# Two-layer adaLN network: gates fixed on columns, row spreading per element, and the seam into attention rearranged

## The chip, the cores and the metric

The kernel runs on one core of one Trainium2 chip. The metric is the device time of one execution in microseconds (us), as the median of several runs. The engines are TensorE (PE; its weight loads are shown as PEld), VectorE (DVE), ScalarE (ACT), GpSimd (POOL) and SyncE (SP, which here only issues transfers). Each runs its own list of instructions in order, and they wait for one another through semaphores.

## What is computed

Eight batch elements of 512 tokens with 128 channels pass two blocks. All numbers are float32.

```
mod = (silu(c) @ wmod).reshape(8, 6, 1, 128)          # for each layer: sa, ca, ga, sb, cb, gb
ga  = (2*(ga >= 0) - 1) * maximum(abs(ga), 0.25)      # the same for gb: "fixing" a gate
# layer 0
h = layernorm(x)*(1 + ca) + sa;  x = x + ga * rwkv(h)              # time mixing, WKV scan over 512 tokens
h = layernorm(x)*(1 + cb) + sb;  x = x + gb * (quant(h) @ quant(W).T + bias)   # 6-bit blocks of 32
# layer 1
h = layernorm(x)*(1 + ca) + sa;  x = x + ga * attention(h)
h = layernorm(x)*(1 + cb) + sb;  x = x + gb * tanh(x_t @ wo.T + c_final @ uo.T + bo)
```

The attention has 16 heads in four groups of four. Each query sees three sets of keys: latent keys (causal), 32 tokens selected by the highest score of `h @ w_imp`, and "window" keys (causal). Three gates per element, a softmax over the mean of `h @ w_gate`, weight the three. Part of each query and key is rotated (rope).

## The kernel before

**Setup.** SyncE loads the weights. TensorE forms `mod` with channels on partitions (`modc`, 12 rows of 8 elements). Layer 0 also needs gates and shifts as rows, the same on all partitions. For that TensorE multiplies, for each of the eight elements, silu(c) repeated over 128 columns with the modulation weights (L1612 to L1618); ScalarE copies 4x128 columns to `modrow` (`row_read`, L814) and VectorE copies layer 1's output gate to `garow1` (`row_reads`, L1159). VectorE then fixes the gates in their row form by `row_gates` (L1166): four passes over 8x128 columns each for `modrow[:, :, 0]`, `modrow[:, :, 3]` and `garow1`; `ffn_rows` (L1171) adds one and forms the bias row `brow` for all elements.

**Layer 0.** A loop written out over b = -2 to 9 on each engine holds element b+1 in its mixing part, b in its WKV part, b-1 in its FFN and b-2 in its passage to attention. VectorE's order in a step is: `wkv(b)` (starts with the scan at L1212, ends with the product at L1232), `quantised_ffn(b-1)` (ends with the codes at L1089), `maxima(b+1)`, `norm_ffn(b)`, `keep_moments(b-2)`, moments of `norm_mix(b+2)`, `norm_attention(b-1)` (L1247). ScalarE: `normed_mix(b+1)` (L820), `mix_input(b+1)` (L836), `normed_attention` and `attention_input(b-2)`, `receptance(b+1)` (L842), `ffn_input(b-1)`, `exponentials(b+1)` (L848 to L854), `normed_ffn(b)`. GpSimd: `gate_wo(b)` (L638), `decode(b-1)` (L651), deviations (L625 to L632), `modulate_ffn(b)`, `gate_ffn(b)`. TensorE: transposes (L1623), projections (L1639, L1640), `project_out` (L1648), `ffn` (L1661, L1666), one score row (L1679).

Into this loop a table `SLOTS` (L107) places the projections of attention's first group, which all pass one shared PSUM bank: each `fill` on TensorE waits for the `read` of the one before. The top-32 choice of elements 0 to 3 is made in step 6; reading the rank, normalising the tokens (`tokens`, L1293) and picking (L1298) follow in step 7, `ks`, the projection of selected keys and its rotation (L1318 to L1327), in step 8. GpSimd rotates the first group's keys (`rope(start, "k", 0)`, L663 to L676) in step 7, ahead of step 8's `decode(7)`. Steps 8 and 9 end element 7: its FFN, normalisation, passage, score, the three gate products (`gate_logits`, L1855) and `vs`.

**Transfers.** SyncE moves rotated and other parts to the group buffers in an order written out by hand: queries' rotated halves, unrotated queries, rotated window keys, unrotated window keys, latent keys (`lay_group`, 28 transfers, 32 with the shared key), then `lay_selected` (12). Both queries' and keys' rotated parts count on one semaphore, `s_lx`.

**Attention.** A unit is one head and one or two tiles of queries against one key set; 24 units make a group: 12 on latent and selected keys, 12 on window keys. `Turn(FIRST)` is group 0 of element 0, then a hardware loop runs seven full turns of four groups and a last one of three. In a unit TensorE makes scores (L1822), VectorE masks and finds the maximum (L1425), ScalarE exponentiates (L980), TensorE transposes (L1849), VectorE or ScalarE moves the result, TensorE multiplies with the values (L1783). In the first turn TensorE waits at unit 0 for all transfers of the group; VectorE waits before it for all GpSimd steps of layer 0 (L1550). `FIRST` also holds the top-32 choice of elements 4 to 7 (from unit 2 on) and the softmax of the gates.

## Time and profile before

| | |
|---|---|
| median of 3 runs | 2014.3 us (2013.28 to 2017.04) |
| profiled execution: time, span | 2014.44 us, 2012.6 us |
| TensorE busy | 1822.4 us (91%) |
| VectorE busy | 1287.3 us (64%) |
| ScalarE busy | 1173.0 us (58%) |
| GpSimd busy | 677.5 us (34%) |
| mean granted clock of TensorE | 0.947 |

Rows of a time line give the start in us from the span's start, the duration in us of the merged instructions, the engine, the line of the kernel, the operation, output and input names and sizes, the count, and in brackets the idle time before and what ended it. Names such as `arena` cover many buffers; the line tells which. Rows of the table by stage give the stretch, its length, then the busy us (and instructions) of PE, PEld, DVE, ACT and POOL, the granted clock of TensorE as a share of 2.4 GHz, the share of the DMA engines and GB/s. The profile has one execution only, on the one core.

### The profile page before, as it was taken

The page shows a single profiled execution, that of the slowest core. Times are in us where ns is not written, and L with a number is a line of the kernel's source. Part 1 is how long each engine was busy: PE and PEld are TensorE (multiplying, and loading weights), DVE is VectorE, ACT ScalarE, POOL GpSimd, SP SyncE. Part 2 cuts the span into 40 slices and gives each one's busy share as a digit, 9 for nine tenths or more (in the row PEclk, how much of TensorE's full clock was granted, in tenths as well). Part 3 has the DMA queues.
Part 4 walks back from the last instruction along what each step waited for, and adds up shares of the span by engine and source line. Part 5 has one row for each costly group of instructions (what it writes and reads, how often), then busy time and mean ns, then how long its engine had stood idle before and what let it go on. Part 6 is the DMA issues. An engine that isn't in the chain of part 4 may idle for free.

```text
span 2012.6 us, 38380 instructions
## 1 busy us (share of the span) xinstructions
PE 1822.4 (91%) x10672; PEld 1076.1 (53%) x10672; DVE 1287.3 (64%) x3817; ACT 1173.0 (58%) x3572; POOL 677.5 (34%) x698
## 2 busy tenths in 40 slices
PE   5575789999999999999999999999999999999996
PEld 3332445555555555655555555555655556555552
DVE  6999666656566666666666656665666666666672
ACT  3464356656565656666565656665666566666651
POOL 1456433343233323333343333332333234333300
PEclk8778589999999999999999999999999999999998
DMA  4001021111011111121112111120111111211101
GB/s 157 1 0 27 15 58 38 38 43 52 24 40 39 47 35 38 42 48 48 39 38 52 48 26 47 35 54 20 44 43 38 49 38 38 52 48 38 37 1 42
DMA packets 71346, 81.42 MB, mean 40 GB/s; under 512 B 29521, under 2 KB 37842, under 8 KB 70994
## 3 DMA queue, kind: packets, MB, share of 16 engines
q1 hardware_dynamic: 71122, 78.74, 15.4%
q8 instruction: 103, 1.69, 0.4%
q14 instruction: 121, 0.99, 0.2%
HBM read 7.90 MB, written 2.10 MB: 5 GB/s over the span
## 4 chain that ended last, share of the span: by engine, by line
issue 49%; PE 21%; POOL 19%; DVE 8%; ACT 2%; POOLq 1%; DMA 0%; DVEq 0%; SPq 0%; ACTq 0%
PE bank L1822 6%; PE bank L1849 3%; POOL arena L674 3%; PE bank L1783 3%; POOL arena L676 3%; POOL arena L663 2%; POOL arena L673 2%; POOL arena L664 2%; PE bank L1688 2%; POOL arena L672 1%; POOL arena L712 1%; DVE arena L1225 1%; PE bank L1683 1%; PE bank L1746 1%; PE bank L1729 1%
## 5 line engine op out<-in xcount | busy, mean ns | idle before, releaser
L1425 DVE CUSTOM_DVE_ANT_0 arena<-bank,W 128x512 f32<-128x512 f32 (+3 forms) x1024 | 480.6, 488 | 523.0 <-PE bank L1822 363.9
L980 ACT ACTIVATE arena<-arena 128x512 f32<-128x512 f32 (+3 forms) x1024 | 570.4, 560 | 369.5 <-DVE arena L1425 366.6
L1822 PE MATMUL bank<-arena 96*128 96x512 f32 (+6 forms) x2048 | 716.5, 452 | 15.9 <-issue 14.5
L1822 PEld LDWEIGHTS bank<-arena 96*128 96x128 f32 x2048 | 350.2, 192 | 190.5 <-issue 154.5
L1849 PE MATMUL bank<-W,arena 128*128 128x128 f32 x2560 | 430.0, 282 | 0.1
L1849 PEld LDWEIGHTS bank<-W,arena 128*128 128x128 f32 x2560 | 301.4, 144 | 222.1 <-issue 183.3
L1436 DVE COPY arena<-bank 128x512 f32<-128x512 f32 (+1 forms) x512 | 318.5, 622 | 78.6 <-PE bank L1849 75.8
L712 POOL TENSOR_TENSOR arena<-arena,one 128x512 f32<-128x512 f32 x64 | 66.8, 1044 | 812.2 <-DVE arena L1393 806.2
L1783 PE MATMUL bank<-arena 128*32 128x256 f32 (+1 forms) x3072 | 223.2, 363 | 1.9 <-DVE arena L1436 1.8
L980 ACT ACTIVATION_READ_ACCUMULATOR arena<-arena 128x1 f32 x1024 | 197.3, 193 | 0.0
L959 ACT ACTIVATE arena<-bank 128x384 f32<-128x384 f32 x256 | 124.6, 487 | 94.4 <-PE bank L1849 92.6
L1783 PEld LDWEIGHTS bank<-arena 128*32 128x32 f32 x3072 | 61.0, 108 | 184.8 <-issue 158.9
L663 POOL TENSOR_TENSOR arena<-arena,W 128x512 f32<-128x512 f32 x64 | 69.9, 1092 | 205.4 <-ACT arena L898 205.4
L974 ACT ACTIVATE arena<-bank 128x32 f32<-128x32 f32 (+1 forms) x384 | 65.2, 205 | 105.0 <-DVE arena L1425 103.8
L1688 PE MATMUL bank<-arena,W 128*128 128x512 f32 x192 | 103.1, 619 | 21.9 <-ACT arena L898 21.8
L1687 PE MATMUL bank<-arena,LW 96*128 96x512 f32 x192 | 103.3, 620 | 2.8 <-ACT arena L898 2.7
L672 POOL TENSOR_TENSOR arena<-arena 128x512 f32<-128x512 f32 x64 | 81.4, 1272 | 56.1 <-DMA arena<-arena 50.0
L1623 PE MATMUL bank<-W,arena 128*128 128x128 f32 x160 | 34.0, 351 | 71.6 <-ACT arena L820 45.3
L898 ACT ACTIVATE arena<-bank 128x512 f32<-128x512 f32 x128 | 76.2, 595 | 33.4 <-PE bank L1687 19.4
L1425 DVE DVE_READ_ACCUMULATOR2_ANT arena<- 128x1 f32 x1024 | 84.8, 83 | 0.0
L676 POOL TENSOR_TENSOR arena<-arena 128x512 f32<-128x512 f32 x64 | 81.3, 1270 | 5.0
L674 POOL TENSOR_TENSOR arena<-arena,W 128x512 f32<-128x512 f32 x64 | 78.0, 1220 | 0.0
(265 smaller groups left out, 2221.0 us busy)
## 6 DMA issues: line engine op xcount, KB each, us to landing
arena<-arena SPq DMA_DIRECT2D x896, 64.0 KB, 2.0
arena<-arena SPq DMA_DIRECT2D x64, 128.0 KB, 2.6
W<-wide SPq DMA_DIRECT2D x1, 3730.0 KB, 13.4
X<-x SPq DMA_DIRECT2D x8, 256.0 KB, 5.5
out<-arena SPq DMA_DIRECT2D x8, 256.0 KB, 2.3
arena<-arena SPq DMA_DIRECT2D x96, 16.0 KB, 1.9
LW<-lat SPq DMA_DIRECT2D x1, 768.5 KB, 14.3
arena<-mods SPq DMA_DIRECT2D x1, 768.0 KB, 4.5
```

Of the source, the lines that this page charges most:

```text
L663: step(pool.tensor_tensor(rt[:, 2], rt[:, 0], w("cos"), ALU.mult))
L674: step(pool.tensor_tensor(rt[:, 1], rt[:, 1], w("cos"), ALU.mult))
L676: pool.tensor_tensor(stX2, rt[:, 0], rt[:, 1], ALU.add).then_inc(s_rope, 1)
L959: A(turned(turn, k), turned_bank(turn, k), ACT.Copy).then_inc(s_pa, 1)
L980: done = A(here, here, ACT.Exp, bias=nmax[:, c:c + 1], scale=-1.0, accum_out=lsum[:, c:c + 1])
L1425: last = v.tensor_tensor_reduce(Pb[:, s % 4, at_p:at_p + n], bank[turn.score_bank(s)][:, at + lo:at + lo + n], w("mask", T - n), -1.0, 3e3 ...
L1436: CP(turned(turn, k), turned_bank(turn, k)).then_inc(s_pd, 1)
L1687: return MM(dst[:], LW[0:QL, col:col + P], latT[0:QL], start=True, stop=True)
L1688: return MM(dst[:], w("wink", col, P), hTc, start=True, stop=True)
L1783: last = MM(bank[5][rows, low * 2 * P:low * 2 * P + n], V[a][turn.g(q) % 2][:, c, rows], PT[low][:, h, c * 2 * P:c * 2 * P + n], start=(c ...
L1822: last = MM(B_[:, at:at + lo + n], query(t), Kb[a][g % 2][0:QD, h, skip:skip + lo + n], start=True, stop=True)
L1849: last = pe.transpose(bank[3 + k % 2][:, n * P:(n + 1) * P], Pb[:, k % 4, c * P:(c + 1) * P], ident)
```

## The change

Three groups of edits.

1. Gates. VectorE fixes the gates in `modc` (columns 2, 5, 8 and 11 at once, 4x8 columns) and forms `brow` there with channels on partitions; the bias weight is a new column of the packed weights, so its own transfer goes. The eight row products of the setup, `row_reads`, `row_gates` and `ffn_rows` go. `rows(b)` on TensorE now spreads one element's four columns through products with the identity (eight passes of 128 columns), for element 0 before the loop and for b+1 at the end of step b; `modrow` has two places in place of eight. ScalarE's `row_read(b)` follows `mix_input(b+1)`. `garow1` is spread in two halves in steps -1 and 0 (`output_gates`), read by ScalarE. The FFN's bias comes from `brow` times the identity.
2. Seam. The loop ends at b = 8. Element 7's last normalisation, its transposes (`z3T`), the scores of elements 4 to 7 (`score`), the gate products (`gates`) and `vs` become tasks of the first attention turn, at units 2, 4, 7 and 12; the top-32 choice there starts at unit 6 in place of 2, and the rank moves from 14 to 17. The slots of steps 6 to 8 change: rank at the end of 6, selected tokens and keys at the top of 7, `x2k`, `nk3`, `nk1`, `vl` after them.
3. Rotation. `rope(start, "k", 0)` moves behind `decode(7)` in step 8. SyncE lays the first group's selected keys, latent keys and then rotated keys; `s_lx` is split in two, and TensorE waits for the window keys only at a group's unit 12.

```diff
-        extra = [(14, "rank")] if first else [(12, "z4T"), (14, "gf"), (15, "gi"), (19, "gc")]
+        extra = [(2, "z3T"), (4, "score"), (7, "gates"), (12, "vs"), (17, "rank")] if first else [(12, "z4T"), (14, "gf"), (15, "gi"), (19, "gc")]
...
-         (6, "mid"): "vw", (6, "out"): "x1k", (6, "end"): "x2k",
-         (7, "mid"): "rank", (7, "out"): "nk3", (7, "end"): "sel",
-         (8, "top"): "ks", (8, "out"): "nk1", (8, "end"): "vl", (9, "out"): "vs"}
+         (6, "mid"): "vw", (6, "out"): "x1k", (6, "end"): "rank",
+         (7, "top"): "sel", (7, "next"): "ks", (7, "out"): "x2k", (7, "end"): "nk3",
+         (8, "top"): "nk1", (8, "mid"): "vl"}
...
@@ SyncE
-            lay_group(Turn(START), 0)
+            lay_queries(start, 0)
+            lay_latent_queries(start, 0)
             sp.wait_ge(s_ksd, 1)
             lay_selected()
+            lay_latent_keys(start, 0)
+            lay_keys(start, 0)
...
@@ GpSimd
                 if 0 <= b < B:
-                    if b == 0:
-                        pool.wait_ge(s_rowg, 1)
+                    pool.wait_ge(s_rowsa, b + 1)
                     gate_wo(b)
                 if 0 <= b - 1 < B:
                     decode(b - 1)
+                if b == B:
+                    rope(start, "k", 0)
...
-                if b == 7:
-                    rope(start, "k", 0)
...
@@ ScalarE
             def row_read(b):
                 act.wait_ge(s_rows, b + 1)
-                A(modrow[:, b].rearrange("p a c -> p (a c)"), bank[4 + b % 2][:], ACT.Copy).then_inc(s_rowsa, 1)
+                if b > 1:
+                    act.wait_ge(s_wdg, b - 1)
+                A(modrow[:, b % 2].rearrange("p a c -> p (a c)"), bank[4][:], ACT.Copy).then_inc(s_rowsa, 1)
...
+                    if turn.first and s == 1:
+                        normed_attention(B - 1)
...
-            for b in range(5):
-                row_read(b)
             act.wait_ge(s_setup, 1)
-            normed_mix(0)
-            for b in range(5, B):
-                row_read(b)
-            for b in range(-2, B + 2):
+            row_read(0)
+            for b in range(-2, B + 1):
                 if 0 <= b + 1 < B:
-                    if b + 1 > 0:
-                        normed_mix(b + 1)
+                    normed_mix(b + 1)
                     mix_input(b + 1)
+                if 0 < b < B:
+                    row_read(b)
+                if 0 <= b < 2:
+                    output_gates(b)
...
@@ VectorE
-            gate_fix(modc[:, 11], gmx, gsm)
             step.settle()
-            TS(gsm, gmx, 1.0, None, ALU.mult).then_inc(s_setup, 1)
+            gate_fix(modc[:, 2:12:3], ta, tb)
+            step.settle()
+            step(TS(brow, modc[:, 5], vec("b0"), None, ALU.mult))
+            step.settle()
+            CP(cells[:, 1:2], cells[:, 0:1]).then_inc(s_setup, 1)
...
-            for b in range(-2, B + 2):
-                if b == -1:
-                    row_gates(modrow[:, :, 0])
+            for b in range(-2, B + 1):
+                if b == 7:
+                    read(start, "rank", 0)
+                    for j in range(NT):
+                        last = pick(0, j)
+                    last.then_inc(s_zc, 1)
                 if 0 <= b < B:
                     wkv(b)
+                if b == 7:
+                    read(start, "ks", 0)
...
@@ TensorE
-            for b in range(B):
-                if b >= 2:
-                    pe.wait_ge(s_rowsa, b - 1)
-                    pe.wait_ge(s_rowsd, b - 1)
-                MM(bank[4 + b % 2][:], silu[:, b:b + 1].to_broadcast([P, P]), wmod[:, 0, 2 * P:6 * P], start=True, stop=True)
...
+            def spread_rows(dst, columns):
+                for n, column in enumerate(columns):
+                    last = MM(dst[:, n * P:(n + 1) * P], column.to_broadcast([P, P]), ident, start=True, stop=True)
+                return last
+
+            def rows(b):
+                if b > 0:
+                    pe.wait_ge(s_var2, b)
+                spread_rows(bank[4], [modc[:, n, b:b + 1] for n in range(2, 6)]).then_inc(s_rows, 1)
...
-                            pe.wait_ge(s_lx, (p0 + q) * (16 * 4 * HG) + 16 * 4 * HG)
+                            pe.wait_ge(s_lq, (p0 + q) * (16 * 2 * HG) + 16 * 2 * HG)
...
+                        if s % GU == RU:
+
+                            pe.wait_ge(s_lx, (p0 + q) * (16 * 2 * HG) + 16 * 2 * HG)
+                            pe.wait_ge(s_lk, (p0 + q) * (16 * HG) + 16 * HG)
...
-                if 0 <= b - 2 < B:
-                    score(b - 2)
+                if 0 <= b - 2 < HALF_B:
+                    score(bank[5], b - 2).then_inc(s_sc, 1)
+                if 0 <= b < B - 1:
+                    rows(b + 1)
+                if -1 <= b < 1:
+                    output_gates(b + 1)
                 slot(b, "end")
-            gate_logits()
```

## Rows read from the trace of the kernel before

**Rows 1.** busy time by stage (columns: see time and profile)
```profile
64.00:208.00 144.00, 96.53 (x290) 48.23 (x290) 135.12 (x287) 73.76 (x154) 78.45 (x108) 0.75 0.04 10
...
263.66:312.28 48.62, 45.68 (x254) 27.27 (x255) 38.06 (x111) 29.77 (x94) 15.36 (x13) 0.96 0.19 50
```

**Rows 2.** time line of TensorE, unit 24 (start, us, engine, line, out<-in, count)
```profile
312.28 1.02 PE L1822 MATMUL bank<-arena 96*128 96x512 f32 x2
```

**Rows 3.** time line of the setup, GpSimd, ScalarE, VectorE
```profile
16.07 0.20 POOL L632 TENSOR_TENSOR small<-small 128x4 f32<-128x4 f32 x1
...
23.21 1.63 ACT L820 ACTIVATE arena<-X,small 128x128 f32<-128x128 f32 x4
...
37.57 1.04 ACT L854 ACTIVATE arena<-arena 128x1024 f32<-128x1024 f32 x1
...
40.06 1.19 DVE L1212 TENSOR_TENSOR_SCAN arena<-arena 128x512 f32<-128x512 f32 x1
```

**Rows 4.** time line from element 0's WKV scan to element 1's
```profile
43.59 1.65 ACT L820 ACTIVATE arena<-X,small 128x128 f32<-128x128 f32 x4 [4.98 <-POOL small L632]
...
56.16 0.69 DVE L1237 TENSOR_TENSOR arena<-X,bank 128x512 f32<-128x512 f32 x1 [0.72 <-PE bank L1648]
...
59.25 0.66 DVE L1124 TENSOR_SCALAR arena<-garow 128x1024 f32<-128x1024 f32 x1
...
59.30 1.04 ACT L854 ACTIVATE arena<-arena 128x1024 f32<-128x1024 f32 x1
...
63.17 1.22 DVE L1212 TENSOR_TENSOR_SCAN arena<-arena 128x512 f32<-128x512 f32 x1
```

**Rows 5.** time line of element 2's step
```profile
87.68 1.11 PE L1623 MATMUL bank<-W,arena 128*128 128x128 f32 x4 [4.54 <-ACT arena L820]
...
88.84 0.78 ACT L836 ACTIVATE arena<-bank,modc 128x512 f32<-128x512 f32 x1 [1.21 <-PE bank L1623]
...
92.83 0.41 POOL L638 TENSOR_TENSOR arena<-W,arena 128x128 f32<-128x128 f32 x1
...
96.43 0.69 DVE L1232 SCALAR_TENSOR_TENSOR arena<-arena 128x512 f32<-128x512 f32 x1
```

**Rows 6.** time line of VectorE, element 7's step
```profile
208.31 1.19 DVE L1212 TENSOR_TENSOR_SCAN arena<-arena 128x512 f32<-128x512 f32 x1
...
222.44 0.18 DVE L1309 COPY rankT<-bank 128x32 f32<-128x32 f32 x1
...
222.66 1.84 DVE L1293 TENSOR_SCALAR arena<-X,stat 128x128 f32<-128x128 f32 x4
...
224.42 0.67 DVE L1298 TENSOR_SCALAR arena<-W,rankT 128x32 f32<-128x32 f32 x4
```

**Rows 7.** time line from element 7's codes to unit 0 of attention
```profile
234.72 0.69 DVE L1089 TENSOR_TENSOR arena<-arena,small 128x512 fp8e4<-128x512 f32 x1
...
235.95 1.09 POOL L663 TENSOR_TENSOR arena<-arena,W 128x512 f32<-128x512 f32 x1
...
243.01 1.05 POOL L651 TENSOR_TENSOR arena<-arena,small 128x512 f32<-128x512 fp8e4 x1
...
249.27 0.69 DVE L1247 TENSOR_TENSOR X<-arena,bank 128x512 f32<-128x512 f32 x1 [6.31 <-PE bank L1666]
...
251.79 1.02 POOL L630 TENSOR_TENSOR small<-small,cst 128x4 f32<-128x4 f32 x1
...
253.71 8.11 SPq L569 DMA_DIRECT2D arena<-arena  x12
...
263.66 2.05 PE L1822 MATMUL bank<-arena 96*128 96x512 f32 x2 [1.39 <-ACT arena L943]
...
266.04 0.69 DVE L1425 CUSTOM_DVE_ANT_0 arena<-bank,W 128x512 f32<-128x512 f32 x1 [10.99 <-PE bank L1822]
```

**Rows 8.** time line of TensorE, gate products and four transposes of attention
```profile
258.70 3.58 PE L1859 MATMUL bank<-W,hsum 128*128 128x3 f32 x16
...
270.08 0.60 PE L1849 MATMUL bank<-W,arena 128*128 128x128 f32 x4
```

More of the change, by code:

```diff
@@ L665, in rope @@
                 step.settle()
-                use = (turn.p0 + k) * 2 + (0 if kind == "q" else 1)
-                if not (isinstance(use, int) and use == 0):
-                    pool.wait_ge(s_lx, use * (16 * 2 * HG))
+                p = turn.p0 + k
+                use = p * 2 + (0 if kind == "q" else 1)
+                if kind == "k":
+                    pool.wait_ge(s_lq, p * (16 * 2 * HG) + 16 * 2 * HG)
+                elif turn.tasks is not START:
+                    pool.wait_ge(s_lx, p * (16 * 2 * HG))
                 if turn.g(k) == 0 and kind == "q":
@@ L922, in read @@
                     last = A(latT, G[:], ACT.Copy)
+                elif name == "z3T":
+                    last = A(HT[:, (B - 1) * T:], G[:], ACT.Identity, bias=modc[:, 6, B - 1:B],
+                             scale=modc[:, 7, B - 1:B], accum_out=hsum[:, B - 1:B])
+                    last.then_inc(s_ga, 1)
+                    act.wait_ge(s_ga, turn.read("z3T"))
+                    act.sem_inc(s_h3, 1)
+                    return
                 elif name == "vs":
@@ L1306, in read @@
                     v.wait_ge(s_gd, turn.read("o2", k))
+                elif name == "score":
+                    step(CP(top, G[0:B]))
+                    CP(marked, G[0:B]).then_inc(s_gd, 1)
+                    v.wait_ge(s_gd, turn.read("score"))
+                elif name == "gates":
+                    CP(gates[:].rearrange("p b n -> p (b n)"), G[:, 0:3 * B]).then_inc(s_gd, 1)
+                    v.wait_ge(s_gd, turn.read("gates"))
+                    gates_shifted()
                 elif name == "rank":
@@ L1514, in _ @@
                     top_ranked()
+                    for j in range(NT):
+                        tokens(0, j)
                 if 0 <= b - 1 < B:
                     quantised_ffn(b - 1)
-                if b == 7:
-                    read(start, "rank", 0)
-                    for j in range(NT):
-                        tokens(0, j)
-                    for j in range(NT):
-                        last = pick(0, j)
-                    last.then_inc(s_zc, 1)
-                if b == 8:
-                    read(start, "ks", 0)
                 if 0 <= b + 1 < B:
                     maxima(b + 1)
-                if b == -1:
-                    row_gates(modrow[:, :, 3])
-                    ffn_rows()
                 if b == 0:
@@ L1707, in fill @@
                         last = pe.transpose(G[:, j * B:(j + 1) * B], top[:, j * P:(j + 1) * P], ident[0:B, 0:B])
+                elif name == "z3T":
+                    pe.wait_ge(s_z3, B)
+                    last = turn4(G, z3)
+                elif name == "score":
+                    for b in range(HALF_B, B):
+                        last = score(G, b)
+                elif name == "gates":
+                    pe.wait_ge(s_h3, B)
+                    for b in range(B):
+                        last = MM(G[:, 3 * b:3 * b + 3], hsum[:, b:b + 1].to_broadcast([P, P]), w("gate"), start=True, stop=True)
                 elif name == "sel":
@@ L1853, in attend @@
                         fill(turn, *task)
-            def gate_logits():
-                pe.wait_ge(s_h3, B)
-                pe.wait_ge(s_var3, B)
-                for b in range(B):
-                    last = MM(bank[6][:, 3 * b:3 * b + 3], hsum[:, b:b + 1].to_broadcast([P, P]), w("gate"), start=True, stop=True)
-                last.then_inc(s_gl, 1)
             start = Turn(START)
@@ L1867, in slot @@
                     fill(start, name, 0)
-            for b in range(-2, B + 2):
+            rows(0)
+            for b in range(-2, B + 1):
                 if b == 3:
```

179 lines of the change are left out of this document (80 added, 99 removed).

## Prediction

> **What bounds the kernel now.** I read the table by stage first, then the time lines of single engines where it pointed. In layer 0 (64 to 208 us) VectorE is busy 135.1 of 144 us and TensorE 96.5, at a granted clock of 0.75; in the first turn of attention (263.66 to 312.28) TensorE is busy 45.7 of 48.6 us at 0.96 and bounds, with VectorE at 38.1 [rows 1]. Between them lies a stretch in which a chain of single steps runs: VectorE ends its last moments at 251.3 and has nothing of weight until 266.04 [rows 7]. The whole change lies before unit 24 of attention, which starts at 312.28 [rows 2]; the 1700 us behind it have the same work in the same order, so I carry whatever is won at unit 24 to the end. The profiled execution took 2014.44 with a span of 2012.6; the median of the runs shown is 2014.3, so a saving is taken off either alike.
>
> Let element b be one of the eight batch elements, and "W(b)" the start of its WKV scan on VectorE (L1212). Four points carry the sum: W(0) 40.06 [rows 3], W(1) 63.17 [rows 4], W(7) 208.31 [rows 6], unit 24.
>
> **Setup, W(0).** Before, TensorE spreads eight elements' gates one after another, and ScalarE normalises element 0 only after five row copies, at 23.21, though its deviation was ready at 16.27 [rows 3]. After it, one element is spread (four columns in two passes of 128 each, about 2 us: an estimate from twice the 1.11 of four transposes of 128 columns in one pass each, cold [rows 5]; it begins at 13.3 and is done before the normalisation) and one copy of 0.6 follows. VectorE's four fixing steps now cover 4x8 columns in place of 8, and one small product and a copy replace the last step: +0.3. So the normalisation starts at 16.6 and ends at 18.3. From there to the last exponential I take element 1's chain, in which TensorE was at 0.5: its normalisation started at 43.59 and took 1.65, its last exponential ended at 60.34, 15.1 later [rows 4]. W(0) is then at 33.4: 6.7 won. Element 0's own chain in the old kernel, mostly at the upper clock, took 13.8 from 24.84 to 38.61, 1.6 of which was waiting behind row products: 12.2, W(0) at 30.5, 9.6 won. I take the cold value, since TensorE will have stood for some 3 us before the transposes, and after 4.5 us of standing the transposes at 87.68 took 1.11, where four of them in attention take 0.60 [rows 5, 8].
>
> The Trainium skill (TensorE: Matmul & The Clock Gate, section HAM oscillation) says that a stream of matmuls which pauses between bursts falls back to the lower clock. By that rule 33.4 is right and the spread products are no lasting warm-up; without it W(0) would be 30.5. The trace agrees in kind: the granted clock is 0.75 over layer 0 [rows 1].
>
> **Gates of the rows, W(1).** The fixing of the output gates (four passes over 1024 columns and a marker, 59.25 to 63.17) goes: 3.9 [rows 4]. The two fixings of modrow and the bias product fall into the stretch already counted, up to W(0). The 0.72 for which VectorE waited before 56.16 for element 0's projection goes too [rows 4], since TensorE is done sooner. Is something else late then? W(1) on VectorE would be 33.4 + (59.25 - 40.06 - 0.72) = 51.9; element 1's exponentials end 16.75 after its normalisation begins [rows 4], which ScalarE can start at 33.4: 50.2. VectorE stays last by 1.7. W(1) moves by 6.7 + 3.9 + 0.7 = 11.3.
>
> **Elements 1 to 6.** Each step gains on TensorE eight passes (2.1 cold), behind the projection and FFN of the element, waiting for the FFN moments; on ScalarE a copy of 0.6; VectorE has nothing new. Behind the waiting TensorE stand only the next element's transposes, whose input comes over 4 us later from GpSimd and ScalarE (normalisation of element 2 after VectorE's moments: 1.25 + POOL + 1.65). On ScalarE the copy stands behind mix_input and before receptance, which waits for r, three projections of 512 columns later. On GpSimd gate_wo now waits at the head of a step for that copy, with decode behind it: in element 2's step mix_input ended at 89.6, so the copy at 90.2; gate_wo ran at 92.83 [rows 5]. Cost nothing, with 2.6 us of cover, and more for decode, whose codes come after rwkv; if the cover is gone it costs what the copy is late. No row shows the pair, so I bound it at -0.5 to +0.5 per step, six steps: -3 to +3. I take 0, VectorE being 94% busy.
>
> **Element 6's step, W(7).** The tokens (1.84) move from element 7's step to this one; reading the rank (0.18) and the picks (0.67) move ahead of W(7) [rows 6]. TensorE reaches the rank transposes only after the FFN, the spread of element 7 (2) and ScalarE's read of a key projection; VectorE in the meantime has the residual addition and moments, 2.0 by the piece from 249.27 to the deviation whose third step is at 251.79 [rows 7]: a wait of 0.8, estimated from 2 + 0.6 + 0.2 - 2.0. Together 3.5 later. W(7) is 208.31 - 11.3 + 3.5 = 200.5.
>
> **End of layer 0.** In times of the old trace from W(7) on: rank, tokens and picks (222.44 to 225.0, [rows 6]) go, the selected keys' rotation comes in their place (seven operations of 128 columns; by the 0.2 to 0.67 of the picks and of such a row 2 to 3, taken as the same 2.6); its 24 products now run under the WKV scan. So element 7's codes end at 235.41 as before. Decode then no longer queues behind the key rotation (from 235.95): it starts at 235.9 in place of 243.01 [rows 7]. From decode's start to the last residual addition took 6.26 (249.27); but TensorE must first do nk1, the last-but-one transposes and vl, each cold: walking these, I get 245.8 and not 242.2. The moments are then at 247.8. GpSimd meanwhile rotates the keys (7.0, to 243.9; more if VectorE is in its way) and makes the deviation, whose last counted step ended 1.53 after the moments (at 252.81). VectorE still waits for all GpSimd steps before attention: it starts unit 0 at 249.4 in place of 266.04. The old start hung on SyncE: the transfers that needed the rotated keys came first, then from 253.71 the 12 of the selected keys, on whose copy unit 0 waited [rows 7]. After: the selected keys are ready at about 223 (rank's 222.44, less some 2 of the quantisation ahead of it, plus 2.6), their 12 issues (8.1) end at 231, the latent keys follow nk1's read at 236.7 and have landed by 241.5. The rotated keys' 12 transfers (0.67 each) follow rotation from 243.9 to 252; unit 12 needs them some 25 us after unit 0. So TensorE starts unit 0 at 245.8, right behind the last FFN, in place of 263.66, and stands two to three units ahead of VectorE.
>
> **First attention turn.** It takes over z3T, four scores, the gate products and vs. At the upper clock: score pairs like unit 24's pair of 512 columns, 1.02 each, 3.9 with overlap [rows 2]; 16 gate products at half of the cold 3.6; z3T and vs at most like four transposes, 0.60, and half of it [rows 8]: together 6.5. TensorE stood 2.9 us in this turn [rows 1], so little hides; the least is 6.5 - 2.9 = 3.6, the most (all at 1.2 GHz) 13. On ScalarE a normalisation of 1.65 stands before the exponentials of unit 1: +1. Ranking moves four units later, with one unit and not two before the rank transposes. The old turn lasted 48.6 from TensorE's start and 46.2 from VectorE's. From 245.8: 245.8 + 48.6 + 6.5 = 300.9; from 249.4: 249.4 + 46.2 + 6.5 + 1 = 303.1. I take 302. Unit 24 comes 10.3 before 312.28 on the old clock, on top of the 7.8 by which W(7) moves.
>
> **Sum.** 11.3 - 3.5 + 10.3 = 18.1 won. Span 1994.5; time 2014.3 - 18.1 = 1996.2.
>
> **Rivals.** (1) The moved work costs double in the first turn: it waits for element 7's chain, VectorE (38.1 of 48.6 us busy there [rows 1]) and the late rank, or runs at the lower clock. 7 us less: 2003. For it: little slack of either engine; against: a granted clock of 0.96 over this turn. (2) All short ends: setup warm (2.9), TensorE's clock up at the end of layer 0 so that the last addition is at 242.2 (3.6), waits of the turn filled (2.9): 9.4 more, 1987. (3) The change doesn't do what it says at the start of attention: VectorE's wait for all GpSimd steps, or a transfer, holds unit 0 so that half of the 17 us stays: 2004.5. (4) Slower: the row copy in front of gate_wo and decode. If the copy ends later than rwkv (96.43 + 0.69 in element 2's step) TensorE's projection waits, and each us is paid in seven steps. Copy end to rwkv is 6.9 us; gate_wo takes 0.4 of it. From 6.5 + 18.1/7 = 9.1 us of delay per step the kernel is slower than before; with 10.5 us (a copy stuck behind the exponentials) it is 7 x 4.0 - 18.1 = 9.9 slower, 2024. Against: ScalarE is in order and has nothing long between mix_input and the copy.
>
> **How the numbers follow.** Forecast (1991 to 2000) 0.55; (1) 0.17; (2) 0.13; (3) 0.09; (4) 0.03; a rest of 0.03 for no net change. The range is 1987 to 2005: it takes in (1) to (3) and the bounds of the spread. Some 0.2% (4 us) is what a measurement of this kernel can tell from no change. Faster 0.93, within 0.04, slower 0.03.
>
> **What would show it.** W(0) at 33 (30.5 if warm), W(1) at 52, W(7) at 200, VectorE's unit 0 at 249.4 - 7.8 = 241.6, unit 24 at 294; periods between W(1) and W(6) unchanged within 0.5; no wait of TensorE for GpSimd's L638 in steps 1 to 7; SyncE's selected-key transfers ahead of the rotated keys. I am wrong if the first turn lasts over 60 us, if the step periods grow, or if the groups after unit 24 change.

## The result, and the profile after

The changed kernel takes 2029.07 us (2025.57 to 2031.45, five runs) against 2014.3 of the kernel before (2010.06 to 2020.21, five runs): the ratio is 1.0068, 95% interval 1.0045 to 1.0091. It is slower; I had forecast 1996.2. The profiled execution took 2025.57 with a span of 2023.5, 10.9 more than before. Three executions among the later runs took far longer (8660 us in e1, 5094 in e11, 2328 of the kernel before beside e9 to e12) and are in no ratio.

The seam came out nearly as forecast. The time lines of VectorE and TensorE after, at the starts of the WKV scans of elements 0, 1 and 7, unit 0 on either engine, and unit 24:

```profile
33.18 1.23 DVE L1227 TENSOR_TENSOR_SCAN arena<-arena 128x512 f32<-128x512 f32 x1 [5.40 <-ACT arena L877]
51.42 1.19 DVE L1227 TENSOR_TENSOR_SCAN arena<-arena 128x512 f32<-128x512 f32 x1
...
199.71 1.22 DVE L1227 TENSOR_TENSOR_SCAN arena<-arena 128x512 f32<-128x512 f32 x1
...
234.96 1.54 PE L1846 MATMUL bank<-arena 96*128 96x512 f32 x2
...
239.09 0.69 DVE L1447 CUSTOM_DVE_ANT_0 arena<-bank,W 128x512 f32<-128x512 f32 x1 [1.88 <-issue]
...
295.85 1.02 PE L1846 MATMUL bank<-arena 96*128 96x512 f32 x2
```

The same points of the kernel before are 40.06 [rows 3], 63.17 [rows 4], 208.31 [rows 6], 263.66 and 266.04 [rows 7] and 312.28 [rows 2]. Unit 24 comes 16.4 us sooner. Then the gain is lost and more. This is the table by stage, one row for each full turn of attention, counted from VectorE's first instruction in it (columns: stretch, length, busy us of PE, PEld, DVE, ACT and POOL, granted clock, DMA share, GB/s), of before:

```profile
313.29:528.43 215.14, 205.30 (x1281) 122.61 (x1280) 132.75 (x414) 133.32 (x421) 72.89 (x68) 0.99 0.17 42
528.43:743.48 215.05, 205.51 (x1276) 122.98 (x1272) 132.64 (x413) 133.20 (x421) 72.89 (x68) 0.98 0.17 42
...
sum 1699.31, PE 1606.27 PEld 957.07 DVE 1038.36 ACT 1030.22 POOL 546.77; mean PE 200.78 PEld 119.63 DVE 129.79 ACT 128.78 POOL 68.35
```

and of after:

```profile
296.85:511.68 214.83, 203.59 (x1274) 121.76 (x1274) 133.70 (x415) 133.20 (x422) 79.12 (x68) 0.99 0.17 42
511.68:729.96 218.28, 207.36 (x1273) 123.64 (x1273) 133.75 (x413) 133.32 (x421) 79.12 (x68) 0.98 0.17 41
...
1387.46:1607.56 220.10, 208.06 (x1273) 123.65 (x1272) 133.86 (x413) 133.20 (x421) 79.14 (x68) 0.97 0.17 41
...
sum 1726.65, PE 1619.18 PEld 961.73 DVE 1047.84 ACT 1030.24 POOL 593.38; mean PE 202.40 PEld 120.22 DVE 130.98 ACT 128.78 POOL 74.17
```

From the start of the first full turn on, the same work takes 27.3 us more (1726.65 against 1699.31). Two things stand in these rows. GpSimd is busy 79.1 us a turn in place of 72.9, with as many instructions (68). And the first full turn is as quick as before, every later one 3.2 to 5.2 us longer, which points at the loop's jump back (this holds for one of the two causes only: in e7 below the first full turn is long too). For 12.9 of the 27.3 us TensorE is busy with the same matmuls, so it ran at the lower clock more often; for 14.4 it stands.

### The profile page after: what moved, and what is told of

The parts are those of the page before. It is cut to its first block, busy times and chain, and to the rows that moved or that the text cites. A ratio compares the mean times of both kernels' runs of the same rounds, so it can differ in the third digit from the quotient of the medians.

```text
span 2023.5 us, 38502 instructions
## 1 busy us (share of the span) xinstructions
PE 1825.5 (90%) x10720; PEld 1083.9 (54%) x10720; DVE 1280.0 (63%) x3786; ACT 1173.5 (58%) x3574; POOL 724.3 (36%) x698
## 4 chain that ended last, share of the span: by engine, by line
issue 47%; PE 20%; POOL 19%; DVE 1%; ACT 1%; POOLq 1%; DVEq 0%; ACTq 0%
PE bank L1846 6%; PE bank L1873 3%; POOL arena L693 3%; POOL arena L692 3%; POOL arena L680 3%; PE bank L1806 3%; POOL arena L695 2%; POOL arena L679 2%; PE bank L1701 2%; POOL arena L731 1%; POOL arena L691 1%; PE bank L1696 1%; PE bank L1769 1%; PE bank L1752 1%; POOL arena L717 1%
## 5 line engine op out<-in xcount | busy, mean ns | idle before, releaser
L1846 PE MATMUL bank<-arena 96*128 96x512 f32 (+6 forms) x2048 | 721.2, 454 | 14.5 <-issue 14.5
L1846 PEld LDWEIGHTS bank<-arena 96*128 96x128 f32 x2048 | 353.1, 193 | 190.7 <-issue 154.6
L1806 PE MATMUL bank<-arena 128*32 128x256 f32 (+1 forms) x3072 | 227.4, 364 | 2.7 <-issue 1.4
L1806 PEld LDWEIGHTS bank<-arena 128*32 128x32 f32 x3072 | 62.2, 109 | 188.8 <-issue 164.0
L679 POOL TENSOR_TENSOR arena<-arena,W 128x512 f32<-128x512 f32 x64 | 81.6, 1276 | 191.6 <-ACT arena L921 191.6
L921 ACT ACTIVATE arena<-bank 128x512 f32<-128x512 f32 x128 | 76.2, 595 | 44.9 <-PE bank L1700 29.8
L691 POOL TENSOR_TENSOR arena<-arena 128x512 f32<-128x512 f32 x64 | 81.4, 1272 | 48.1 <-DMA arena<-arena 42.8
L693 POOL TENSOR_TENSOR arena<-arena,W 128x512 f32<-128x512 f32 x64 | 89.1, 1392 | 0.0
## 6 DMA issues: line engine op xcount, KB each, us to landing
W<-wide SPq DMA_DIRECT2D x1, 3730.0 KB, 13.4
LW<-lat SPq DMA_DIRECT2D x1, 768.5 KB, 14.3
```

The costliest lines, as they stand in the source:

```text
L679: step(pool.tensor_tensor(rt[:, 2], rt[:, 0], w("cos"), ALU.mult))
L693: step(pool.tensor_tensor(rt[:, 1], rt[:, 1], w("cos"), ALU.mult))
L1806: last = MM(bank[5][rows, low * 2 * P:low * 2 * P + n], V[a][turn.g(q) % 2][:, c, rows], PT[low][:, h, c * 2 * P:c * 2 * P + n], start=(c ...
L1846: last = MM(B_[:, at:at + lo + n], query(t), Kb[a][g % 2][0:QD, h, skip:skip + lo + n], start=True, stop=True)
```

## Two suspects in code that the change never touched

**GpSimd's rotations.** Groups of GpSimd by line from 500 to 1600 us (count | busy us, mean ns | idle before), before:

```profile
L672 POOL TENSOR_TENSOR arena<-arena 128x512 f32<-128x512 f32 x40 | 50.9, 1272 | 34.3 <-DMA arena<-arena 30.2 <-POOL arena L664 4.1
L663 POOL TENSOR_TENSOR arena<-arena,W 128x512 f32<-128x512 f32 x40 | 43.7, 1092 | 127.1 <-ACT arena L898 127.1
```

and after:

```profile
L679 POOL TENSOR_TENSOR arena<-arena,W 128x512 f32<-128x512 f32 x40 | 51.0, 1276 | 121.1 <-ACT arena L921 121.1
L691 POOL TENSOR_TENSOR arena<-arena 128x512 f32<-128x512 f32 x40 | 50.9, 1272 | 32.0 <-DMA arena<-arena 28.6 <-POOL arena L680 3.4
```

Three of the four products of a rotation, which read cosines or sines from the packed weights W, went from 1092 to 1276 ns, and the fourth from 1204 to 1385; the subtraction, which reads two of the rotation's own buffers, stayed at 1272. From the start of the first product to that of the second it is 1050 ns before and 1234 after, so this is more than a way of recording. Nothing in those lines was edited. But the bias became an eleventh column among the vectors of W, and every column behind it, cosines and sines too, moved by 4 bytes. ScalarE's read at L921 fills the rotation's buffers, so it comes after the rotation before it; TensorE waits for that read 20.4 us in this window, in place of 13.5.

VectorE has one operation that slows down as well, a sum of two buffers that reads nothing of W (before, after):

```profile
L1408 DVE TENSOR_TENSOR arena<-arena 128x512 f32<-128x512 f32 x20 | 15.4, 769 | 0.0
L1430 DVE TENSOR_TENSOR arena<-arena 128x512 f32<-128x512 f32 x20 | 21.7, 1083 | 0.0
```

It makes up most of the 9.5 us by which VectorE is busier in the sums above. The half of its instructions that run beside one of GpSimd's products went from 0.84 to 1.35 us. It is hardly what costs the time: in the fastest version of all, e15, it takes 1107 ns. Why it slows down is open.

**TensorE behind the jump.** The time line of TensorE over the start of the second full turn. Before:

```profile
738.53 0.55 PE L1849 MATMUL bank<-W,arena 128*128 128x128 f32 x3
741.27 1.48 PE L1822 MATMUL bank<-arena 96*128 96x512 f32 x2 [2.20 <-issue]
742.69 1.08 PE L1783 MATMUL bank<-arena 128*32 128x256 f32 x8
```

After:

```profile
725.01 0.55 PE L1873 MATMUL bank<-W,arena 128*128 128x128 f32 x3
727.77 2.07 PE L1846 MATMUL bank<-arena 96*128 96x512 f32 x2 [2.22 <-issue]
729.77 0.64 PE L1806 MATMUL bank<-arena 128*32 128x256 f32 x1
730.56 1.08 PE L1806 MATMUL bank<-arena 128*32 128x256 f32 x7 [0.16 <-issue]
```

Each jump back costs a stand (2.2 us here, 2.2 to 2.8 at the six jumps) in which TensorE waits for nothing that the profile shows. Behind it the kernel before runs on; the changed one does three matmul passes and stands once more, though the eight passes of L1806 are issued in one go. The queues of the DMA section that load instructions (packets, MB) say what it is. Before, after:

```profile
q8 instruction: 103, 1.69, 0.4%
```

```profile
q8 instruction: 110, 1.80, 0.4%
```

## Experiments

**e1 to e4: the offset alone.** Unused columns behind the vectors move the rest of W, here for e1 (e2: before with 11, e3: after with 12, e4: before with 12 columns in all):

```diff
-WIDE = [("c", 2 * B), ("vecs", 11), ("ident", P), ("wkT", P), ("wvT", P), ("wrT", P), ("woT", P), ("ffn", P),
+WIDE = [("c", 2 * B), ("vecs", 26), ("ident", P), ("wkT", P), ("wvT", P), ("wrT", P), ("woT", P), ("ffn", P),
...
+    cols += [np.zeros((P, 15), np.float32)]
     cols += [np.eye(P, dtype=np.float32)]
```

> The changed kernel with 15 unused columns behind the eleven vectors of the packed weights W: every later column of W lies 64 bytes further than in the kernel before, and not 4 bytes as in the changed kernel. Theory A (offset of the operands: the one added column moved the cosines and sines by 4 bytes, and GpSimd's products with them went from 1.092 to 1.276 us): the products take 1.09 again, a full turn of attention lasts 215 us in place of 218 to 220, the group sequence is the old one and the 16.4 us won at unit 24 reach the end: 1997 to 2000 us. Rival B (the split waits of TensorE and the new order of SyncE's transfers slow the turns): turns stay at 218 to 220 and the time at 2029. Rival C (other places of the stage buffers or of the code): as B.

> The kernel before with one unused column behind the ten vectors of W, nothing else: the 4 byte shift alone. Theory A: GpSimd's products with cosines and sines take 1.276 in place of 1.092 us, full turns last 218 to 220 in place of 215, and the kernel takes 2036 to 2046 us. Rivals B and C: 2014 us, turns 215.

> The changed kernel with one more unused column: later columns of W are 8 bytes further than before. Open which alignment matters. If GpSimd reads in words of 8 bytes (A8): products 1.09 and 1997 to 2000 us. If operands must share a place within a line of 16 or 64 bytes (A64): products stay at 1.27 and the time at 2029. Rivals B and C: 2029, with 1.09 or 1.27 alike.

> The kernel before with two unused columns: 8 bytes. A8: products 1.09, 2014 us. A64: products 1.27, 2036 to 2046. Rivals B and C: 2014.

| kernel | shift of W | product L663/L679 | full turns 2 to 6 | us | ratio to before |
|---|---|---|---|---|---|
| after | 4 B | 1276 ns | 218.3 to 220.1 | 2029.07 | 1.0068 (1.0045 to 1.0091) |
| e1 after | 64 B | 1093 ns | 217.6 to 219.2 | 2010.01 | 0.9989 (0.9975 to 1.0003) |
| e2 before | 4 B | 1274 ns | 213.7 to 220.3 | 2039.25 | 1.0134 (1.0117 to 1.0151) |
| e3 after | 8 B | 1272 ns | 219.6 to 222.1 | 2032.03 | 1.0089 (1.0064 to 1.0115) |
| e4 before | 8 B | 1272 ns | 218.5 to 220.7 | 2041.31 | 1.0147 (1.0129 to 1.0166) |

The one column makes the kernel before 1.3% slower by itself: theory A is right about its cause, and words of 8 bytes are not the rule. But e1 is not the 1997 to 2000 that I expected. Its products are quick again, its first full turn takes 213.5 us, and the next ones still 217.6 to 219.2. The second stand is there, at 1.0 to 1.4 us behind three of the six jumps and 0.2 to 0.4 behind the other three:

```profile
723.44 0.55 PE L1873 MATMUL bank<-W,arena 128*128 128x128 f32 x3
726.12 1.12 PE L1846 MATMUL bank<-arena 96*128 96x512 f32 x2 [2.13 <-issue]
727.17 0.45 PE L1806 MATMUL bank<-arena 128*32 128x256 f32 x1
728.91 1.08 PE L1806 MATMUL bank<-arena 128*32 128x256 f32 x7 [1.29 <-issue]
```

**e5 to e8: the place of the loop.** Instructions that only raise an unused semaphore, ahead of TensorE's first wait:

```diff
+            for _ in range(20):
+                pe.sem_inc(s_pad, 1)
             pe.wait_ge(s_silu, 1)
```

> The changed kernel with the 64 byte shift of the 64B run, and 20 instructions on TensorE that only raise an unused semaphore, issued while TensorE waits for the first data. The 64B run had GpSimd's products at 1.09 us again, but its full turns behind the first still lasted 217 to 219 us: behind each jump back of the attention loop TensorE stands for 2.1 us, as before, then does three matmul passes, stands again for 1.0 to 1.3 us with no releaser, and runs at the lower clock for up to 11 us. Theory D (code place: TensorE's loop begins 12 instructions ahead of the end of a block of instruction memory, so that a second block must be fetched after the jump; the added instructions before the loop moved it there): 20 more instructions put the loop's start 8 into a block; the second stand goes, full turns last 213.5 to 215 us, 1995 to 1999 us in all. Rival E (the split waits or SyncE's order make the turns longer): as the 64B run, 2010 us.

> The kernel before with 89 such instructions on TensorE ahead of its first wait: its attention loop then begins at the same instruction number as the changed kernel's. Theory D: a second stand of about 1.2 us behind each jump back, turns 217 to 219 from the second on, GpSimd's products at 1.09, 2014 + 6 x 2 to 3 = 2024 to 2034 us. Rival E: 2011 us, turns 215.

> The changed kernel with the 20 instructions on TensorE alone (cosines and sines still 4 bytes off). Theories A and D together: GpSimd's products 1.276, no second stand, 2029 less what the stand cost (12 to 18 us): 2011 to 2017 us. If the two costs don't add, up to 2029.

> The kernel before with 25 such instructions: the loop's start stands at the same place within blocks of 64 instructions as in the changed kernel, and at another within blocks of 128 or 256. A second stand behind the jump (turns 217 to 219): blocks of 64. None (turns 215, 2011 us): blocks of at least 128.

e5 takes 1994.81 us, ratio 0.9937 (0.9917 to 0.9958): the second stand is gone, q8 has 104 packets, and the turns are those of before within 1 us, the sixth is 2.0 shorter (time line of TensorE behind a jump, then the row of the third full turn):

```profile
724.00 1.17 PE L1849 MATMUL bank<-arena 96*128 96x512 f32 x2 [2.36 <-issue]
725.10 1.08 PE L1809 MATMUL bank<-arena 128*32 128x256 f32 x8
```

```profile
726.08:941.07 214.99, 205.65 (x1277) 123.24 (x1274) 132.56 (x413) 133.19 (x421) 72.89 (x68) 0.98 0.17 42
```

e6, the reverse, takes 2031.82, ratio 1.0104 (1.0080 to 1.0128), with 109 packets in q8, six more than before, one for each jump. Not all of it is the loop: the 89 instructions hold TensorE's first matmul until 14.42 us (6.42 before), and the first full turn starts 6.6 later (319.91 against 313.29). From there to the end it takes 1710.4 us against 1699.3: 11.1 for the place of the loop, as in e1 (1711.2). The second stand is seen behind three of the six jumps (0.7 to 1.3 us). e8 took 2013.47 in one run, with 103 packets and turns of 214.9 to 216.8 and no second stand, so the blocks are larger than 64 instructions.

e7 misses the 2011 to 2017: 2018.92, ratio 1.0052 (1.0035 to 1.0070). That is 0.2% better than the changed kernel, with intervals that overlap, where e5 is 0.5% better than e1. The traces, one execution of each version, show the two costs side by side, from the start of the first full turn to the end, for e1 (the loop's place alone) and e7 (the offset alone):

```profile
297.35:2008.50 1711.15, 1613.54 (x9903) 958.24 (x9902) 1038.93 (x3216) 1030.26 (x3245) 547.00 (x509) 0.98 0.16 40
296.69:2015.90 1719.21, 1615.34 (x9903) 966.62 (x9902) 1047.22 (x3216) 1029.30 (x3244) 592.75 (x509) 0.98 0.16 40
```

With neither (e5) it is 1697.8 us, with both (the changed kernel) 1726.6. So the loop's place alone costs 13.4, the offset alone 21.4, and both together 28.9 and not 34.8: the two costs don't add in full. The offset needs no jump: e7's first full turn takes 218.0 us where e5's takes 216.1. At the jump shown above, TensorE came into the changed kernel's loop at the lower clock (L1846 took 2.07 us and not 1.12), so that the second block arrived before it was needed but for 0.16 us; the stand was covered by slowness that was paid for anyway. That is how it goes in general: the fourth pass behind a jump starts 2.5 to 2.9 us after the first at all six jumps of the changed kernel and of e1, and 1.1 to 2.0 us after it in the kernel before, e5 and e7. How much of this is seen as a stand depends on the clock of the three passes.

**The clock behind a stand.** The granted clock behind the jump shown, in windows of 2 us of the kernel before (columns as above):

```profile
741.00:743.00 2.00, 1.73 (x6) 0.50 (x10) 0.00 (x0) 0.00 (x0) 0.00 (x0) 0.72 0.06 16
743.00:745.00 2.00, 2.00 (x12) 1.03 (x5) 1.12 (x4) 0.42 (x1) 0.00 (x0) 0.50 0.01 4
745.00:747.00 2.00, 2.00 (x13) 0.71 (x12) 0.84 (x4) 0.99 (x3) 1.04 (x1) 0.92 0.00 0
```

and the first and last windows of the low stretch in e1:

```profile
727.00:728.00 1.00, 0.63 (x2) 0.14 (x2) 0.00 (x0) 0.00 (x0) 0.00 (x0) 0.70 0.02 8
...
737.00:738.00 1.00, 1.00 (x10) 0.34 (x10) 0.70 (x2) 0.00 (x0) 0.00 (x0) 0.68 0.07 16
```

Before, the clock is at its lower level for 3.4 us (2 x (0.28 + 0.50 + 0.08) = 1.7 us of work at full clock); in e1, with a second stand of 1.3 us, for three times as long, 5.1 us of work. So at this jump the stand came with up to 3.4 us more of lost clock. Other jumps differ: the stretch is 3.4 us at four of the six jumps before and 6.8 at the other two, 6.8 at four jumps of e1 and 10.2 at two, and 3.4 at all six of e5. From the first full turn to the end e1 has TensorE busy 7.2 us longer than e5 and standing 6.2 us longer.

**e9: which offset.** A probe behind the last transfer of the kernel before, with the other engines done, 40 lines of this form with other offsets each:

```diff
+                after_one(TTp(at(2048, 0), at(0, 0), at(1024, 1), ALU.mult))
```

> The kernel before, and behind its last transfer a probe on GpSimd alone, with every other engine done: products of two 128x512 float arrays, each line with one set of offsets of the two inputs and the output, in floats from three bases that stand at the same place of a 64 byte line, 4 times each. Adds some 250 us at the end, which only the probe takes. If the relative place of the inputs decides (R): offset 6 of the second input (the 24 bytes that cosines stood from the staging buffers in the kernel before) takes 1.09 us, 7 and 8 and 0 take 1.27, and (6, 6) takes 1.27 like (0, 0). If the place within a line of one input alone decides (S): the first input's offset or the second's changes it, and (6, 6) is like (0, 6). If neither is seen with the engines idle, it was contention with another engine (C): all lines take the same.

Groups of GpSimd by line; second input at offset 0, 1, 2, 3, 4 and 7 floats (L816 to L823), first input at 1 and 2 (L833, L834), output at 2 (L841), both inputs at 6 (L847):

```profile
L816 POOL TENSOR_TENSOR arena<-arena 128x512 f32<-128x512 f32 x4 | 5.0, 1262 | 0.3
L817 POOL TENSOR_TENSOR arena<-arena 128x512 f32<-128x512 f32 x4 | 4.4, 1091 | 0.3
L818 POOL TENSOR_TENSOR arena<-arena 128x512 f32<-128x512 f32 x4 | 4.4, 1091 | 0.3
L819 POOL TENSOR_TENSOR arena<-arena 128x512 f32<-128x512 f32 x4 | 5.0, 1262 | 0.3
L820 POOL TENSOR_TENSOR arena<-arena 128x512 f32<-128x512 f32 x4 | 5.0, 1260 | 0.3
L823 POOL TENSOR_TENSOR arena<-arena 128x512 f32<-128x512 f32 x4 | 5.0, 1262 | 0.3
L833 POOL TENSOR_TENSOR arena<-arena 128x512 f32<-128x512 f32 x4 | 5.0, 1258 | 0.3
L834 POOL TENSOR_TENSOR arena<-arena 128x512 f32<-128x512 f32 x4 | 4.4, 1092 | 0.3
L841 POOL TENSOR_TENSOR arena<-arena 128x512 f32<-128x512 f32 x4 | 5.0, 1262 | 0.3
L847 POOL TENSOR_TENSOR arena<-arena 128x512 f32<-128x512 f32 x4 | 5.0, 1262 | 0.3
```

R holds. All 40 lines obey one rule: with the second input 1 or 2 floats ahead of the first modulo 4 floats (16 bytes), the product takes 1.09 us; at 0 or 3 it takes 1.26 (from start to start 1.17 and 1.34). The output's place plays no part, and the difference is the same with the other engines idle. In the kernel before the cosines stood 6 floats on (2 modulo 4, quick); the bias column made it 7, one more makes 8, both slow. One or two columns more leave the buffers behind W where they are: in the compiled program of the kernel before W ends 8 bytes short of the next buffer.

**e10, e11, e13: no jump at all.** The attention loop written out seven times, on TensorE (e10), on all engines (e11), and on all engines in the kernel before (e13):

```diff
-            with pe.Fori(0, B - 1) as i:
+            for i in range(B - 1):
```

> The changed kernel with the 64 byte shift and TensorE's attention loop written out seven times, no jump: theory D taken to its end. Each of six jumps cost a stand of 2.1 us and, behind it, 3.4 us at the lower clock (1.7 us of work), in e5 as in the kernel before. If fetching without a jump is hidden and no other engine's own jump takes its place: 1994.8 - 6 x 3.8 = 1972. If the other engines' jumps (VectorE and ScalarE still loop) hold TensorE nearly as long: 1985 to 1995. If straight code of 24000 instructions is fetched too slowly: over 1995, with stands everywhere.

> The same with the attention loop written out on all five engines. Theory D to its end: 1968 to 1974 us, no stand at the turn's boundary. If the fetching of all five engines' code gets in the way of each other or of the transfers: over 1980.

> The kernel before with the attention loop written out on all five engines, as in e11 for the changed one. Theory (the change wins 16 to 19 us ahead of unit 24 and nothing behind it): 1973 + 18 = 1991 us (1988 to 1993), and the difference to e11 at the end is that at unit 24. Rival (the changed kernel's turns are better or worse by themselves too): the difference grows or shrinks from turn to turn.

e10: 1988.3, ratio 0.9881 (0.9852 to 0.9909); TensorE's stands turned into waits for VectorE, which still jumps (waits of VectorE, 500 to 1600 us: total, times, longest):

```profile
DVE gtc L1586 <- issue: 15.9, 6, 2.7
```

e11: 1973.28, ratio 0.9810 (0.9781 to 0.9839), full turns of 209.9 to 213.5 and no stand, as theory D has it. e13: 1982.12, ratio 0.9859 (0.9833 to 0.9884), better than the 1988 to 1993 expected. So the change is worth 0.5% here, by ratios whose intervals just overlap. By the profiled executions the changed kernel is 15.0 us ahead at the start of the first full turn (296.92 against 311.94) and 9.8 at the end (1970.7 against 1980.5): 5 us go on the way. From that start on TensorE does the same 9903 passes in 1594.5 us of busy time against 1590.6: 3.9 of the 5.2 are the lower clock. This pair was to show whether the turns are worth the same in both kernels; the difference shrinks, as the rival said.

**e12 and e16: two terms of the sum.** e5 with the rotation back in front of the decoding, and e5 with TensorE's wait for the rotated and window keys back at a group's first unit:

```diff
-                if b == B:
-                    rope(start, "k", 0)
...
+                if b == 7:
+                    rope(start, "k", 0)
```

```diff
-                        if s % GU == RU:
+                        if s % GU == 0:
```

> The 64 byte, 20 instruction version with one edit undone: GpSimd rotates the first group's keys before the last element's decoding, as in the kernel before. Theory (the decoding is on the path at the end of layer 0, as the prediction has it): decode starts 5 to 7 us later, TensorE's unit 0 and the end move by 4 to 7 us: 1999 to 2002 us. Rival (the first turn waits for the ranks later on and takes it up): 1995 to 1997.

> The 64 byte, 20 instruction version in which TensorE waits for the rotated keys' transfers ahead of a group's first unit, as in the kernel before, and not ahead of its thirteenth. In e5 these transfers were issued until 253.2 and unit 0 began at 232.3. Theory of the prediction (the split lets unit 0 start early): unit 0 at about 255, the end 10 to 20 us later: 2005 to 2015. Rival (the first turn's wait for the ranks and its other work hide it): under 2000. Later groups have their keys long before, so turns stay at 215.

e12: 1997.92, ratio 0.9940 (0.9924 to 0.9956), between my two numbers, and not to be told from e5's 0.9937. In its trace unit 0 is 4.5 us later than in e5 (236.79 against 232.28) and unit 24 6.3 later (299.68 against 293.41), but e5 then spends 3.4 us of work at the lower clock in its first full turn where e12 loses 1.7. The order of rotation and decoding is worth 0 to 3 us at the end, which these runs can't tell from nothing. e16: 2005.4, ratio 0.9977 (0.9960 to 0.9994): the split is worth 0.4%. TensorE stands at unit 0:

```profile
241.44 2.04 PE L1849 MATMUL bank<-arena 96*128 96x512 f32 x2 [8.54 <-DMA arena<-arena]
```

I had expected unit 0 at 255: I read the end of a merged row of 24 transfers, of which the last belong to the next group.

**e14, e15: the rule used.** The second and fourth of the rotation's four buffers 4 bytes further on, so that all six operations are of the quick kind, in e5 (e14) and in e11 (e15):

```diff
-        rt = cv(4, T)
+        rt_a, _, rt_b, _, rt_c, _, rt_d, _ = (cv(n) for n in (T, 1, T, 15, T, 1, T, 15))
+        rt = (rt_a, rt_b, rt_c, rt_d)
```

> The 64 byte, 20 instruction version with the second and the fourth of GpSimd's rotation buffers 4 bytes further on, so that in every operation of a rotation the inputs stand 4 or 8 bytes apart modulo 16. By the probe's rule all six operations take 1.09 us: L692's and L696's subtraction and addition fall from 1.27, a rotation is 0.36 us shorter. If each 0.18 us is worth what the four products' 0.18 were worth (3.3 us a turn for 0.74 us a rotation): up to 1.6 a turn, 1983 us. If a rotation at 7 us is already early enough for TensorE: 1994 to 1995.

> The same buffers in the changed kernel with all loops written out (e11): the fastest version that the runs point to. 1973 less 0 to 12: 1961 to 1973.

```profile
L693 POOL TENSOR_TENSOR arena<-arena 128x512 f32<-128x512 f32 x41 | 44.8, 1092 | 31.3 <-DMA arena<-arena 28.2 <-POOL arena L682 3.1
L697 POOL TENSOR_TENSOR arena<-arena 128x512 f32<-128x512 f32 x41 | 44.7, 1091 | 3.2
```

Subtraction and addition take 1.09 in place of 1.27 (e14). e14: 1988.18, ratio 0.9885 (0.9869 to 0.9902), 0.5% better than e5. e15: 1964.76, ratio 0.9763 (0.9746 to 0.9779), the fastest version, 2.4% below the kernel before. e14 falls between its two expectations (1983, and 1994 to 1995), e15 inside its range.

## Why the prediction was wrong, point by point

- **W(0), W(1).** Forecast 33.4 and 52, measured 33.18 and 51.42. That W(0) fits this well is in part luck: the normalisation starts 0.6 us late (17.22), and from its end to the last exponential it takes 14.3 us, not the 15.1 of a cold chain or the 12.2 of a warm one. Of the six pairs of projection passes the first two are cold (2.08 and 1.82 us), the other four take 1.02.
- **Elements 1 to 6.** Forecast as before within 0.5 a step. W(1) to W(6) took 111.4 us (110.5 before): +0.8, inside the bound of -3 to +3. Single steps differ by -0.8 to +0.9, more than the 0.5.
- **W(7).** Forecast 200.5, measured 199.71; the step grew by 2.3, not 3.5.
- **Unit 0.** Forecast (with the 7.8 taken off) 238.0 on TensorE and 241.6 on VectorE, measured 234.96 and 239.09. The walk through the end of layer 0 was 3 us too long: 0.8 stood at W(7), 1 more at the end of element 7's codes (225.80 against 227.6), 1 behind them. That unit 0 stands on the split wait is shown by e16 (241.44 against 232.28 in e5).
- **First turn.** From TensorE's unit 0 to unit 24 forecast 56.2 (302 less 245.8), measured 60.9: the term that was mis-sized at the seam, by 4.7. The moved work itself was sized rightly (1.06 + 3.60 + 1.95 + 0.43 = 7.0 us of passes for 6.5). But TensorE stands 6.5 us in this turn in place of the 2.9 of before, where I had let no wait come in, and some 2 us more of work are lost to the lower clock. The two waits are 3.1 us for a read that ScalarE makes behind unit 0's exponentials, which hang on VectorE's late start at 239.09, and 2.8 us for the late ranks (the turn, then the two waits):

```profile
234.96:295.85 60.89, 54.40 (x292) 31.98 (x292) 38.92 (x122) 33.23 (x104) 19.18 (x22) 0.94 0.20 53
...
241.18 1.13 PE L1700 MATMUL bank<-arena,LW 96*128 96x512 f32 x2 [3.12 <-ACT arena L921]
...
282.44 0.38 PE L1720 MATMUL bank<-W,arena 8*128 8x8 f32 x4 [2.84 <-DVE arena L1303]
```

- **Unit 24.** Forecast 18.1 sooner, measured 16.4, and 18.9 in e5 (293.41). Of the rivals, (1) comes nearest: waits for VectorE and the late ranks, priced at 7 us where the turn was 4.7 longer. Against it stands the second part of (2), an earlier last addition: 235.21, where I had 238.0 and the rival 234.4, though not by the clock as it says. (3) is seen only in the 3.1 us above. Of (4) there is one wait of 2.5 us for `gate_wo`, at 180.68, where the kernel before stands 3.4 us.
- **The carry to the end. This step failed:** "the 1700 us behind it have the same work in the same order, so I carry whatever is won at unit 24 to the end". Same work and order they have, and 27.3 us more time. I looked at what the change edits and not at what it shifts. The runs show in its place two costs that I had put at nothing: the 4 byte shift of cosines and sines (21.4 us alone, e7 against e5) and the new place of TensorE's loop (13.4 alone, e1 against e5). The column `("vecs", 11)` was in the diff, and I noted it only as a transfer that goes; the longer list of TensorE ahead of the loop was there too, and I gave it no term.
- **Shown for it:** both shifts undone, e5 gives 1994.81, 1.4 us from the forecast. In ratios, the forecast was 0.9910 and e5 is 0.9937 (0.9917 to 0.9958): of 18 us some 13 arrive, and in the pair e11, e13 some 10. The profiled executions say it differently: e5 is 18.9 us ahead at the first full turn and 20.4 at the end, but that execution of the kernel before (2014.44) is slower than the medians beside the experiments (2009.4 to 2012.2). So between 10 and 20 us arrive, and these runs do not say more. The agreement of 1994.8 with 1996.2 is in part luck: the runs of before beside e5 had a median of 2009.4.

Two of the three marks of being wrong that I had written came: the first turn lasts over 60 us (60.9), and the groups after unit 24 change.

How the two costs share the 27.3 us is given by the traces of e1, e5 and e7 only up to their overlap of some 6 us. By the ratios the offset costs 1.2% with the loop well placed (e7 against e5) and 0.8% with it badly placed (after against e1); the loop's place 0.5% and 0.2% (the last not clear of noise). Why the clock falls once in one turn and twice in another is open.

## What to carry to other kernels

A change costs what it moves, not only what it edits. Before carrying a gain through untouched code, list what shifts under it: the address of each operand behind a new column or buffer, and the place of each loop behind a longer list of instructions. When untouched work turns slower, compare its mean durations by line, and the packets of the instruction queues, before looking for a new wait; and test a change again at another offset before calling it bad.

## What the runs showed of the hardware

- GpSimd's product, sum or difference of two 128x512 float32 arrays took 1.09 us with the second input 4 or 8 bytes ahead of the first modulo 16, and 1.26 to 1.28 otherwise, with all other engines idle too. (One product of a rotation, L674 or L693, is an exception: 1.20 and 1.39.) Four bytes of shift cost the kernel before 1.3% (1.0134).
- A loop's jump made TensorE (some 2890 instructions a turn) stand 2.1 to 2.8 us, and VectorE (762) went on 2.7 to 3.5 us behind its branch; ScalarE, GpSimd and SyncE (655 and fewer) went on 0.2 to 0.3 us behind theirs. With a second block of instructions TensorE's fourth pass came 2.5 to 2.9 us behind the first and not 1.1 to 2.0; behind the jump the clock was at its lower level for 3.4 us or more. Writing out seven turns on all engines saved 1.3 to 1.4% (0.9810 against 0.9937 in the changed kernel, 0.9859 in the one before).
- Instructions that only raise a semaphore took TensorE 0.15 us each: the 89 of e6 run from 0.84 to 14.32 us. They held its first matmul back by 8.0 us only, since it waited until 6.42 before; e5's 20 cost nothing (6.50).
